# One tile of 128 places per expert and a shared tile for the rest of two experts, in a decoder layer with a 48-expert feed-forward

## The reference, cut to what matters

```python
E = gate_up_proj.shape[0]                       # 48
oh = (flat_e[:, None] == jnp.arange(E)[None, :]).astype(jnp.int32)
pos = jnp.sum(jnp.cumsum(oh, axis=0) * oh, axis=-1) - 1
valid = pos < CAP                               # 192
xb = jnp.zeros((E, CAP + 1, H), x.dtype).at[flat_e, pos_c].set(x[tok])[:, :CAP]
gu = jnp.einsum('ech,eoh->eco', xb, gate_up_proj)
g, u = jnp.split(gu, 2, axis=-1)
h = jax.nn.silu(g) * u                          # (E, 192, 192)
out = jnp.einsum('eci,ehi->ech', h, down_proj)  # (E, 192, 512)
final = jnp.zeros_like(x).at[tok].add(out[flat_e, pos_c] * w[:, None])
```

## Time and profile before

| | |
|---|---|
| median of three executions | 943.55 us |
| profiled execution, its own time | 939.5 us |
| span of the profile | 937.6 us |
| busy PE / DVE / ACT / POOL | 840.8 / 631.3 / 400.0 / 466.9 us |
| stage A | to about 340 us |
| stage B and tables | about 344 to 543 us |
| stage C | about 543 to 903 us |
| last norm | about 903 us to the end |

### The profile page before, as it was taken

How to read it: one execution, slowest core, us unless ns; L and a number is a source line. 1 busy time by engine, 2 the same in 40 slices (tenths; PEclk the granted TensorE clock), 3 DMA queues, 4 the chain that set the end, 5 groups by cost and what they waited for, 6 DMA issues and landing times. The chain is left out here.

```text
span 937.6 us, 18549 instructions
## 1 busy us (share of the span) xinstructions
PE 840.8 (90%) x5958; PEld 716.5 (76%) x5959; DVE 631.3 (67%) x1437; ACT 400.0 (43%) x820; POOL 466.9 (50%) x443
## 2 busy tenths in 40 slices
PE   6899999999999889999998779999999999999700
PEld 5677777777777678888887578898998898898600
DVE  6757765677567556777787767676776776766426
ACT  4333233333332412332332046666666666666404
POOL 0242334233433321655555347767777777775354
PEclk9899999999999989999999979999999999999855
DMA  9541112111211026222231959999999999988665
GB/s 338 202 161 46 47 45 89 45 45 45 89 46 34 25 81 200 97 98 95 106 107 68 298 170 260 294 280 289 284 284 275 285 296 285 286 205 197 139 183 210
DMA packets 72509, 155.34 MB, mean 166 GB/s; under 512 B 9888, under 2 KB 10320, under 8 KB 72080
## 3 DMA queue, kind: packets, MB, share of 16 engines
q1 hardware_dynamic: 49888, 99.35, 31.2%
q0 software_dynamic: 22576, 55.42, 24.5%
HBM read 110.22 MB, written 44.52 MB: 165 GB/s over the span
## 5 line engine op out<-in xcount | busy, mean ns | idle before, releaser
L1895 POOL DMA_INDIRECT y_rows<-arena,place_token x96 | 155.9, 1624 | 83.2 <-issue 61.4
L1884 POOL DMA_INDIRECT xg<-x_rows,place_token x96 | 96.7, 1007 | 43.0 <-issue 27.7
L954 PE MATMUL ps<-arena,raw 128*128 128x192 f32 x576 | 100.6, 332 | 5.1 <-DVE arena L1674 4.9
L954 PEld LDWEIGHTS ps<-arena,raw 128*128 128x128 f32 x576 | 96.3, 194 | 7.4 <-issue 5.6
L591 PE MATMUL ps<-w_hi,x_hi 128*128 128x512 f32 (+1 forms) x332 | 79.2, 362 | 10.2 <-ACT arena L991 4.7
L591 PE MATMUL ps<-w_hi,x_lo 128*128 128x512 f32 (+1 forms) x332 | 75.8, 351 | 0.0
L591 PE MATMUL ps<-w_lo,x_hi 128*128 128x512 f32 (+1 forms) x332 | 74.6, 348 | 0.0
L1756 POOL TENSOR_TENSOR arena<-arena,attn_pack 128x512 f32<-128x512 f32 x12 | 16.4, 1367 | 115.9 <-DVE arena L1308 115.9
L954 PE MATMUL ps<-arena,mid_flat 128*128 128x192 f32 x432 | 73.1, 326 | 0.0
L954 PEld LDWEIGHTS ps<-arena,mid_flat 128*128 128x128 f32 x432 | 71.1, 190 | 2.0
L591 PEld LDWEIGHTS ps<-w_hi,x_hi 128*128 128x128 f32 x332 | 53.7, 194 | 21.9 <-issue 9.4
(11 more groups left out here) (231 smaller groups left out, 1970.4 us busy)
## 6 DMA issues: line engine op xcount, KB each, us to landing
raw<-in_gu SPq DMA_DIRECT2D x24, 768.0 KB, 5.1
mid_flat<-in_gu SPq DMA_DIRECT2D x18, 768.0 KB
raw<-in_dn SPq DMA_DIRECT2D x24, 256.0 KB, 6.1
y_rows<-zero SPq DMA_DIRECT2D x20, 256.0 KB, 3.4
mid_flat<-in_dn SPq DMA_DIRECT2D x18, 256.0 KB
arena<-in_gu SPq DMA_DIRECT2D x6, 768.0 KB
arena<-in_xT SPq DMA_DIRECT2D x16, 256.0 KB, 3.2
x_res<-in_x SPq DMA_DIRECT2D x16, 256.0 KB, 2.7
```

The source lines that it names most:

```text
L954: m = pe.matmul(out, wgu[slot][:, q, part * P:(part + 1) * P], xgT[:, p, q, :], start=(q == 0), stop=(q == KC - 1))
L1884: pool.indirect_dma_start(out=xg[:, place, h, :], out_offset=None, in_=x2_d, in_offset=bass.IndirectOffsetOnAxis(ap=place_token[:, 2 * n + ...
L1895: pool.indirect_dma_start(out=y2_d if p and n < DUAL else y_d, out_offset=bass.IndirectOffsetOnAxis(ap=place_token[:, 2 * n + h:2 * n + h ...
```

## The change: what it does, and the diff

The 192 places of an expert are cut in 128 and 64 (`REST`) instead of 96 and 96. The 128 fill a tile; the 64 of experts n and n + 1 (n even) share another.

- Gathers: one indirect DMA of 128 rows per expert, and one of 128 rows per pair.
- Transposes: 8 of 128 rows for an even expert (its tile and the shared one), 4 for an odd one. `copy_x` for an even expert: ACT copies four chunks of 128 columns, DVE the shared rows of both; c_up itself keeps its 12 matmuls of 192 columns.
- Down projection: 5 fp32r matmuls per expert for the 128 places. The shared tile is done once a pair, ahead of the five of the odd expert: two raw fp32 matmuls with 64 stationary columns each, one into PSUM partitions 0 to 63, one into 64 to 127, and one raw fp32 matmul over the whole array for the last 64 inner rows of both (`h_rest`).
- Scaling: ACT scales the even tile and the shared one, DVE the odd one. `ye` has two buffers for even experts, one for odd ones and one shared.
- Scatters: per pair two of 128 rows and two of 64. The even tile goes alone; the two of 64 and the odd tile go together after the odd expert's down projection. `DUAL` is 46.
- SP loads the weights of two experts at a time, once the down projection of the odd one is done (the raw weights are read until then).
- Tables: the first lot has 2 experts, the second 6; each has two spreading matmuls and one more reduction.
- Between B and C: the wait for the seeds moves from the first copy to the first `scale_y`; the last seeds are issued after the first two gathers; one seed that stood ahead of the last flags' scatter moves behind it.
- y2 is read in 8 pieces with two in flight, and each piece of the last norm waits for its own.
- At the end of stage A the low part of the first of the four stage-B weights is made in two halves earlier in DVE's order, and `norm_o` of the last tile goes ahead of `layer_norm1`.

```diff
-HALF = CAP // 2
+REST = CAP - P
+FIRST = 2
-DUAL = 42
+DUAL = 46
...
-            for p in range(2):
-                sp.wait_ge(gu_made[p], (E2 - 4) // 2)
-                sp.wait_ge(dn_split[p], (E2 - 4) // 2)
+            sp.wait_ge(dn_made[1], (E2 - 4) // 2)
             sp.wait_ge(y_added[1], 32 * (DUAL // 2))
-            for q in range(4):
+            for q in range(NT // 2):
+                at_least(sp, y2_in[q % 2], 16 * (q // 2))
...
 def c_turn(p, k, place, lap):
+                pe.wait_ge(got[place], (16 if p else 32) * (lap + 1))
                 for q in range(KC):
-                    for h in range(2):
-                        o = (q % 2) * CAP + h * HALF
-                        m = pe.transpose(ps[:, CT + q // 2, o:o + HALF], xg[:, place, h, q * P:(q + 1) * P], eye[0:HALF, 0:HALF])
+                    bank, o = (CT + q // 2, (q % 2) * P) if p else (CT, q * P)
+                    m = pe.transpose(ps[:, bank, o:o + P], xg[:, place, q * P:(q + 1) * P], eye[:, :])
+                if not p:
+                    for q in range(KC):
+                        m = pe.transpose(ps[:, CT + 1, q * P:(q + 1) * P], xg_rest[:, place // 2, q * P:(q + 1) * P], eye[:, :])
...
-            def c_down(p, k):
+            def c_down(p, k, slot):
-                at_least(pe, y_scaled[1 - p], 2 * (k + p))
-                for h in range(2):
...
+                at_least(pe, y_scaled[p], (p + 1) * k)
+                if p:
+                    for rows, s in ((slice(0, REST), slot - 1), (slice(REST, P), slot)):
+                        pe.matmul(ps[rows, CR, :], h_a[:, s % 4, P:CAP], wdn[s], start=True, stop=False, skip_group_check=True)
+                    pe.matmul(ps[:, CR, :], h_rest[:, slot // 2 % 2, :], rest_at[slot // 2], start=False, stop=True, skip_group_check=True)
+                for i, (lhs, rhs) in enumerate(parts):
+                    m = pe.matmul(ps[:, CY + p, :], lhs, rhs, start=(i == 0), stop=(i == len(parts) - 1))
                 m.then_inc(dn_made[p], 1)
...
+            def scale_y(p, k, slot):
                 act.wait_ge(dn_made[p], k + 1)
+                if p:
+                    at_least(act, y_added[0], 32 * k)
+                    at_least(act, y_added[1], 32 * k)
+                    act.activation(ye_rest[:, :], ps[:, CR, :], ACT.Copy, scale=w_rest[:, slot // 2 % 2:slot // 2 % 2 + 1]).then_inc(y_scaled[1], 1)
+                    return
+                at_least(act, y_added[0], 32 * (k - 1))
...
-            act.wait_ge(y_seeded[0], 16 * (SLOT_T - SLOT_T // 2))
-            act.wait_ge(y_seeded[1], 16 * (SLOT_T // 2))
...
+                dve.tensor_tensor(h_rest[rest_rows[slot], slot // 2 % 2, REST * p:REST * (p + 1)], ps[HI, CG + 1, P:CAP], g_c[HI, P:CAP], ALU.mult)
+                dve.tensor_tensor(h_c[HI, p, :], ps[HI, CG + 1, 0:P], g_c[HI, 0:P], ALU.mult).then_inc(h_made, 1)
...
+            def scatter_pair(k):
+
+                scatter_rest(2 * k)
+                scatter_rest(2 * k + 1)
+                scatter_main(2 * k + 1)
...
             for n in range(E2):
                 if n + 3 < E2:
...
                     c_gather(n + 3)
...
-                if n:
-                    c_scatter(n - 1, *before_it(n % 2, n // 2))
+                if n % 2:
+                    scatter_main(n - 1)
+                elif n:
+                    scatter_pair(n // 2 - 1)
```

More of the change, by code:

```diff
@@ L1183, in c_expert @@
                 act.wait_ge(h_made, 2 * (2 * k + p + 1))
[L1184 removed]
+                act.activation(ha_hi[:, p, :], h_a[:, slot % 4, 0:P], ACT.Copy)
                 act.activation(hc[0:P // 2, p, :], h_c[P // 2:P, p, :], ACT.Copy)
@@ L1880, in c_gather @@
                 at_least(pool, c_turned[p], k - 1)
-                at_least(pool, got[place], 32 * (n // 4))
+                at_least(pool, got[place], (16 if p else 32) * (n // 4))
                 settle(pool)
-                for h in range(2):
-                    pool.indirect_dma_start(out=xg[:, place, h, :], out_offset=None, in_=x2_d,
-                                            in_offset=bass.IndirectOffsetOnAxis(ap=place_token[:, 2 * n + h:2 * n + h + 1].bitcast(U32), axis=0))\
-                        .then_inc(got[place], 16)
@@ new lines, in scatter_rest @@
+            def scatter_rest(n):
+                p, k = n % 2, n // 2
+                pool.wait_ge(y_scaled[1], 2 * (k + 1))
+                if p:
+                    at_least(pool, y_added[1], 32 * k)
+                    if n > DUAL:
+                        pool.wait_ge(y_added[0], 32 * (k + 1))
+                settle(pool)
+                rows = slice(REST * p, REST * (p + 1))
+                to = rows_at(odd_token, REST, k) if p else rows_at(place_token, REST, rest_col(k))
+                pool.indirect_dma_start(out=y2_d if p and n < DUAL else y_d, out_offset=to, in_=ye_rest[rows, :], in_offset=None,
+                                        compute_op=ALU.add).then_inc(y_added[p], 16)
```

247 lines of the change are left out of this document (141 added, 106 removed).

## The result

The changed kernel took 938.04 us (median of 20 runs, 935.4 to 943.86) beside 942.63 us for the kernel before on the same chips: a ratio of 0.9959, 95% interval 0.9945 to 0.9973. The gain is therefore 4 to 6 us. The prediction said 9.4 us by its sum and 933 us. The sign and the range held, and the size is half.

A forecast was written before the change was run, and what follows sets the result against it. PE was taken as the bound, never stopping in stage C. Terms -1.4 - 4 + 0.5 - 4.5 = -9.4 us took 939.5 to 930, 934 against the median; it said 933, range 921 to 956.

The forecast's parts named there:

- The pair of experts: Stage C, PE's work for two experts: 13.69 us after the change against 13.72, -1 us over 24 pairs.
- rival C: Stage C: the two matmuls of 64 columns do not run together, +0.87 us a pair, +21 us, 954 us; chance 0.11.
- The wait for DVE's copy: Stage C: c_up waits for the larger copy ahead of an even expert, 0.3 us a pair (0 to 0.6).
- Stage C: All of stage C: -1 us from 24 pairs and +1.5 for the tables, together +0.5 us.
- the second spreading matmul: Stage C's tables: one more spreading matmul, some 0.3 us for each of 5 groups, +1.5 us.
- Rival B: Stage C: scalings wait for scatters into the odd and shared buffers, a loop longer than a pair; +22 us, 955; chance 0.16.
- End of stage A: Seam before stage B: less DVE work ahead of the last layer norm, -1.4 us (0 to -2.2).
- Between B and C: Seam before stage C: the first copy no longer waits for seeds, -4 us (0 to -6).
- the seed that left GpSimd's queue: Between stages B and C: a seed of 0.96 + 0.30 us no longer precedes the last flags, 1.26 us sooner.
- End of stage C: Tail: only the last two experts' scatters are chained, so y is read sooner; -4.5 us (-2 to -6).
- X + 17.9: Tail: y pieces read 17.9 us after X, the last c_up's end; X + 21 with PE at half speed.
- Rival D: No change: half the overlap of the 64-column matmuls, or seams giving nothing because the next wait takes over; 942 us; chance 0.14.

The follow-up runs named there:

- columns_apart: Changed kernel with the fp32r down products placed between the two raw products of 64 columns: 966.07 us, ratio 1.0236 to the kernel before.
- defer: Changed kernel with DVE copying only the even expert's half of the shared rows ahead, the odd half behind: 930.27 us, ratio 0.9908 to the kernel before.
- again: The changed kernel run once more with no edit: 932.5 us, ratio 0.9938 to the kernel before.
- best: Changed kernel with defer's copy and separate semaphores for the shared tile: 928.12 us, ratio 0.9891 to the kernel before.
- again2: The changed kernel run a further time with no edit: 933.21 us, ratio 0.9946 to the kernel before.

## Why the prediction was right in sign and half wrong in size

*The pair of experts.* Right in mechanism: 13.69 forecast, 13.83 measured. The overlap of the two products is complete (columns_apart), which refutes rival C. The wait for DVE's copy was 0.3 and measured 0.27 to 0.30 (defer). The products of 64 columns take 1.01 us and the third 0.94, together 1.95 where the sum had 0.87 + 0.87 + 0.2 with both switches. The missing 0.14 is mostly c_up: 4.00 + 3.90 us where the sum had 7.80. The Trainium skill, TensorEngine Tiling (Array Packing), section Tiling Modes, says that a change of mode drains the engine; the rows of the pair agree for the way in, since four transposes take 0.53 us to the first product of 64 columns (701.20 to 701.73) and 0.35 to 0.44 us to other work (708.76, 709.20, 709.55): 0.1 to 0.2 us. The way back doesn't stand apart in them. Stage C cost +1.5 us where +0.5 was given, and luck has a part in its being so near. A pair without table work went from 13.74 to 13.83 us, +2.2 over 24 pairs where -1 was given. The +1.5 for the second spreading matmul doesn't show: a pair with table work takes 1.18 us more than the others before (14.92) and 1.17 after (15.00).

*Rival B.* Refuted. PE stays 99.5% busy, and in again ACT waited 6 times, 10.1 us in all, for scatters from 560 to 850 us without PE being late; a second buffer changed nothing.

*End of stage A.* -1.4 was given, and 2.4 us (by all profiles; 3.0 by the first three) came ahead of stage B and 1.0 to 2.3 in its first tile. The term was mis-sized since it counted DVE's work only. What PE gained was a shorter wait for the first gather, and with it a higher clock. The trace before has 0.55 in the first tile (344.56 to 351.61 us), and no row that I had picked held it. This gain wasn't foreseen, and it hides a part of what the tail lost.

*Between B and C.* -4 was given, 2.1 us came. The wait for the seeds went as forecast, and the tables, now in two unequal lots, run 2.7 us longer where I gave 2.4. What failed is the seed that left GpSimd's queue: its 1.26 us show nowhere, for the flags are read 23.3 and 23.4 us after the last tile's transposes before and 23.2 to 23.6 with the change. The wait was also 4.5 us and not 5.2 in the second profile of the kernel before.

*End of stage C: the step that failed.* -4.5 was given and +0.7 came, with +0.6 behind it. The prediction put the chain of the last scatters at X + 17.9 and let the read of y2 run beside it, "so it fits with nothing to spare". The term that was wrong is the length of that read. It starts where the sum had it, 6.6 us after X (10.5 after the last c_up's start), but the last of its eight pieces is asked for 18.0 us after the first, where 4.2 MB at 283 GB/s had given 11. The first piece of y stands behind them on SyncE's queue and follows 0.48 us later. With two pieces in flight the last one has landed 21.5 us after the first request in again, an estimate of 195 GB/s for 4.2 MB.

The scatter times were priced too low as well. I took them from one with nothing else about (4.15 us), and they ran under this read. From the first to the second it is 4.6 to 7.2 us in the ten profiles instead of 4.5, and the last lands 7.2 us after its start in `best`, 0.7 us ahead of the read of y. A resource shown free in the profile before was used by the change itself, for `DUAL` 46 had moved 4.2 MB of reads from 19 us ahead of the last c_up's start to 11 behind it. Half speed of PE, which I had allowed for, came in some executions. PE's last down products end 10.4 us after the start of the last c_up in the first profile and in again, where the sum had 10.6, but 11.8 in again2, at a granted clock of 0.57 from 876 to 880 us. The first scatter then leaves 1.3 us later, and the read of y only 0.3, since the queue holds it.

*Rival D* said that the seams might give nothing because the next wait takes over. That is what happened in the tail, and its 942 is nearly as far from the measured time as the forecast is.

## What to carry to other kernels

When a change moves a large transfer to where a chain of small dependent transfers is, price the small ones by their rows under load, and check what stands behind the large one on its queue. An early gather can be worth more than its wait: here the clock of the work behind it was higher too, fully so in half of the executions. And where two causes of a wait end together, the profile names one; an edit that removes only this one gives nothing.

## What the runs showed of the hardware

- Two fp32 products of 64 stationary columns and 512 moving ones, in column tiles side by side, take 1.01 us together, as one of them does alone.
- A scatter with addition of 64 rows took 4.5 us to the next dependent scatter with nothing else on the queues, and 4.6 to 7.2 us under a 4.2 MB read. One of 128 rows took 5.1 us to the read behind it with nothing else about, and landed 7.2 us after its start under that read.
- 4.2 MB in eight pieces with two in flight, beside three scatters, took 21.5 us from the first request to the last landing (again, first profile).
- TensorE, after 2.7 to 3.6 us of waiting, had a granted clock of 0.53 to 0.55 in the next 7.1 us; after 1.1 to 1.4 us it was 1.00 in six executions and 0.72 in six others. What divides these six from those isn't known.
- Two executions of one kernel differ by up to 3 us in stage B (the other tiles, 142.1 and 145.2 us) and by 1.6 us in one interval of stage C, at a granted clock of 1.00 from 390 to 500 us in both. What makes it isn't known.
